# Moving layer 0's projections, and the place of the row maximum in a slot, in a kernel of two cross-attentions

## The chip, the core and the metric

The kernel runs on one core of a Trainium2 chip. The core has five engines, each with an instruction queue of its own that it works off in order: TensorE (PE: matmuls and transposes), VectorE (DVE), ScalarE (ACT), GpSimd (POOL) and SyncE (SP), which here only issues DMAs. They meet through semaphores. The metric is the time of one execution on the device in microseconds (us), the median of several. Three runs of the kernel before gave 1619.97, 1624.86 and 1628.02 us.

## What is computed

Two layers of cross-attention over the same context: 8 batches, 100 queries of width 512, 722 context rows of width 512. Only layer 0 is touched by the change.

```python
# layer 0 (E=512, 16 heads of 32)
qn, kn, vn = layer_norm(query), layer_norm(key), layer_norm(value)      # key = value = context
Q, K, V = (qn @ wq + bq), (kn @ wk + bk), (vn @ wv + bv)                # split into heads
scores = einsum("bqhd,bkhd->bhqk", Q, K) / sqrt(32)
attn = softmax(scores, axis=-1)
out = einsum("bhqk,bkhd->bqhd", attn, V) @ wo + bo
x = query + out
x = x + gelu(layer_norm(x) @ w1 + b1) @ w2 + b2
# layer 1: the same kind of attention with 16 heads of 64, a constant added to the scores,
# then the output projection, the residual and a layer norm
```

## The kernel before

All matmul operands are held as two float16 parts (a high part and what is left), so that a float32 product is three matmuls. The stages follow one another: the queries of layer 0, attention of layer 0, the MLP, the queries of layer 1, attention of layer 1, the output. The change is in the attention of layer 0, function `attention` with `layer == 0`.

A unit of that attention is one batch. The work is a pipeline over steps s = 0 to 9, each of which has, at the same time, the projections of unit s, the scores and softmax of unit s-1, and the last product and the output of unit s-2. A step is cut into 24 slots (`Slots.n`): 4 groups g of 4 heads, with 6 tiles t of context rows each; slot j = 6g + t. The context of unit s+1 is normalised beside it (`ctx_stats`, `ctx_hi`, `ctx_lo`).

What a slot can hold on TensorE:
- `max_scores` (L821), in slots with t < 4: the scores of one head of the NEXT group, 100 queries by 722 keys, two matmuls into the one buffer `p_max`. VectorE reduces them to the row maximum (`take_max`, L1057); the next `max_scores` waits for that reduction (`max_made`). A "row maximum" below is this pair.
- `scores` (L846): four heads of the present group against tile t, into one of two buffers; ScalarE takes the exponential (L954) and casts it to the high part one slot later (L964), GpSimd makes the low part (L649).
- `max_transposes` (L829), at t = 4: turns the four row maxima, which VectorE has split in two parts behind the last reduction (`split_max`, L1064 and L1066), so that VectorE can copy them into the query stack (`place_max`, L1073). The first `scores` of the next group wait for that copy.
- `times_v` (L872, L873), in slots with t from 2 to 5: one head's product of the probabilities of the previous group with V, 12 matmuls.
- `project` (L799 for K, L804 for V): one of 14 projections (a = 0 to 7 for K, 8 to 13 for V), 12 matmuls into one of two buffers `p_proj`. ScalarE evacuates the high part (`evacuate`, L974 or L982), then VectorE the low part (L1081 or L1087); projection a waits until a-2 is evacuated.
- `out_transposes` (L888) in slot 9, for the output of unit s-2; GpSimd makes its low part (L1230) in slot 8.

Nothing is scheduled by a planner: each engine's function `step` writes its queue in this order, slot by slot. The table `at` says in which slot each projection stands, and `Slots.evac` puts its evacuation into the slot behind it on ScalarE and VectorE. SyncE's queue (loads, the stacking of K by DMA in `stack_k`, context transpositions) is written per unit and waits for evacuations by count. Steps 2 to 5 run in a loop of two passes.

Of the kernel before, what the change touches and what calls it, by code (L numbers as in the profile page):

```python
# [28 lines left out]
KT = -(-SK // P)  # L29
# [12 lines left out]
HG = 4  # L42


MAX_T, PV_T = 4, 2
# [433 lines left out]
class Slots:  # L479
# [4 lines left out]
    def __init__(self, layer):  # L484
        self.layer = layer
        self.groups = 4 if layer == 0 else 2
        self.n = KT * self.groups
        self.heads = HG * self.groups

        at = [0, 1, 3, 4, 6, 7, 9, 10, 12, 13, 15, 16, 18, 21] if layer == 0 else [0, 0, 1, 1, 2, 2, 3, 3, 4, 6, 7, 8, 10, 11]  # L490
        self.proj = [[a for a in range(14) if at[a] == j] for j in range(self.n)]

        self.evac = [(self.proj[j - 1][-1:] if j else []) + self.proj[j][:-1] for j in range(self.n)]
        self.evac[-1] = self.evac[-1] + self.proj[-1][-1:]

        self.stat = {t: t for t in range(KT)} if layer == 0 else {}
        self.var_t = KT
        self.ctx = {8: 0, 10: 1, 12: 2, 14: 3, 16: 4, 18: 5} if layer == 0 else {2: 0, 6: 1, 9: 2}
        self.out_t = 9
        self.units = B if layer == 0 else 2 * B  # L500
        self.per = self.units // B
# [29 lines left out]
def attention(nc, layer, ctx_d, q_d, w_k, w_v, kb_col, vb_row, ident, ident16, eps, score_bias, outT,  # L531
# [12 lines left out]
    sl = Slots(layer)  # L544
    NG, NH, U = sl.groups, sl.heads, sl.units
# [11 lines left out]
    with Scope(nc, f"attn{layer}") as sc:  # L557
# [219 lines left out]
        def _(pe):  # L777
# [47 lines left out]
            def max_transposes(s, G1, g):  # L825

                pe.wait_ge(nm_made, G1)
                misc_wait(s, ("max", g), first=(isinstance(s, int) and s == 0))
                pe.transpose(misc16[:, :SQ], nmax_parts[:SQ, :], ident16[:SQ, :SQ]).then_inc(misc_ready, 1)  # L829
# [51 lines left out]
            def out_transposes(s):  # L881

                pe.wait_ge(o_lo_made, s - 1)
                misc_wait(s, ("out", 0))
                for a in range(2):
                    for k in range(ET):
                        o = (a * ET + k) * P
                        last = pe.transpose(misc16[:, o:o + SQ], oparts[:SQ, a, k * P:(k + 1) * P], ident16[:SQ, :SQ])  # L888
                last.then_inc(misc_ready, 1)

            def step(s, par, b, cpar, kind):
                prep, proj, has_scores, outs = kind
                for j in range(sl.n):
                    g, t = divmod(j, KT)
                    if g < NG - 1 and has_scores and t < HG:
                        max_scores(s - 1, 1 - par, g + 1, t)
                    if g == NG - 1 and proj and t < HG:
                        max_scores(s, par, 0, t)
                    if has_scores:
                        scores(s, s - 1, 1 - par, g, t)  # L900
                    if outs and j == sl.out_t:
                        out_transposes(s)
                    if g < NG - 1 and has_scores and t == MAX_T:
                        max_transposes(s, (s - 1) * NG + (g + 2), g)
                    if g == NG - 1 and proj and t == MAX_T:
                        max_transposes(s, s * NG + 1, g)
                    if 0 <= t - PV_T < HG:
                        if g == 0 and outs:
                            times_v(s - 2, par, NG - 1, t - PV_T)
                        if g > 0 and has_scores:  # L910
                            times_v(s - 1, 1 - par, g - 1, t - PV_T)
                    if proj:
                        for a in sl.proj[j]:
                            project(s, par, cpar, a)
# [117 lines left out]
        def _(dve):  # L1032
# [67 lines left out]
            def out_copy(s, par, b):  # L1100
# [3 lines left out]
                out = outT[0 if layer == 0 else par]  # L1104
                dve.tensor_copy(out[:, :, :, bass.ds(b * SQ, SQ)], src).then_inc(misc_freed, 1)

            def step(s, par, b, cpar, kind):
                prep, proj, has_scores, outs = kind
                for j in range(sl.n):
                    g, t = divmod(j, KT)  # L1110
                    if g < NG - 1:
                        nxt = (s - 1, g + 1) if has_scores else None
                    else:
                        nxt = (s, 0) if proj else None
                    if nxt and t < HG:
                        take_max(*nxt, t)
                        if t == HG - 1:
                            if g > 0:
                                prev = sl.misc_count(s, ("max", g - 1)) if has_scores else None
                            else:  # L1120
                                prev = sl.misc_count(s - 1, ("max", NG - 1))
                            split_max(s, *nxt, prev)
                    if layer == 0 and prep:
                        if j in sl.stat:
                            ctx_stats(s + 1, sl.stat[j])
# [22 lines left out]
                    if proj:  # L1148
                        for a in sl.evac[j]:
                            evacuate(s, par, a)  # L1150
                if layer == 1 and has_scores:
                    prob_lo(dve, s - 1, NG - 1, KT - 1)

# [217 lines left out]
```

## Time and profile before

| | before |
|---|---|
| median of three runs | 1624.86 us |
| the profiled execution | 1620.46 us |
| its span, first to last instruction | 1618.7 us |
| mean granted clock of TensorE, share of full | 0.938 |
| TensorE (matmul) busy over the span | 1389.2 us, 86% |
| VectorE busy | 850.4 us, 53% |
| ScalarE busy | 686.2 us, 42% |
| GpSimd busy | 506.6 us, 31% |

Busy time is over the whole program; what holds in one stage is read from the windows and timelines of that stage. The attention of layer 0 takes about 109 to 592 us of the span. In timelines a line gives start, duration, engine, line and operation, and in brackets how long the engine sat idle before it and what ended that. Durations of instructions that follow each other overlap a little, so a sequence is best measured from start to start. A clock of 1.00 is TensorE's full clock (2.4 GHz), 0.50 its lower level (1.2 GHz).

### The profile page before, as it was taken

The numbers are of one execution on the slowest core, as the hardware profiler recorded it, in microseconds if no ns is written. First come the engines' busy times: TensorE is split into PE (matmuls) and PEld (weight loads), VectorE is DVE, ScalarE is ACT, GpSimd is POOL, SyncE is SP. The second block draws the span as 40 slices with busy tenths as digits, with TensorE's granted clock in tenths as the row PEclk, the third lists the DMA queues.
The fourth block names the chain that finished last, engine by engine and source line by source line (L and its number), as shares of the span: only waits on it lengthen the run. The fifth ranks groups of instructions, "written<-read, shape, count | busy, mean of one in ns | idle before, by whom it ended". The sixth has DMA issues, their size and how long they took to land. (4 is left out here: it accounts for less than half of the span.)

```text
span 1618.7 us, 32652 instructions
## 1 busy us (share of the span) xinstructions
PE 1389.2 (86%) x12428; PEld 867.6 (54%) x12428; DVE 850.4 (53%) x1505; ACT 686.2 (42%) x1358; POOL 506.6 (31%) x580
## 2 busy tenths in 40 slices
PE   5467998889899756999938999999999999999968
PEld 3233555556555532544414666666666566666653
DVE  5735677666655637622343455454455455554544
ACT  1323656465555524421222444444444444444441
POOL 3100555455544655020000222222222222221134
PEclk9787999999999767999979999999999999999979
DMA  4275634444432033110286444444454344442221
GB/s 138 56 151 119 132 79 101 105 95 100 103 80 56 28 94 129 53 59 26 87 224 124 99 97 86 101 101 88 81 95 90 77 98 99 103 86 64 56 82 66
DMA packets 217262, 149.97 MB, mean 93 GB/s; under 512 B 148609, under 2 KB 190081, under 8 KB 217105
## 3 DMA queue, kind: packets, MB, share of 16 engines
q1 hardware_dynamic: 217104, 147.81, 39.1%
q8 instruction: 107, 1.75, 0.5%
q14 instruction: 51, 0.41, 0.1%
HBM read 59.29 MB, written 10.65 MB: 43 GB/s over the span
## 5 line engine op out<-in xcount | busy, mean ns | idle before, releaser
L649 POOL TENSOR_TENSOR attn_probs<-attn_p,attn_probs 128x400 f16<-128x400 f32 (+1 forms) x288 | 273.7, 951 | 677.3 <-ACT attn_probs L964 673.2
L1057 DVE TENSOR_REDUCE attn_nmax<-attn_p_max 100x1 f32<-100x722 f32 x256 | 231.7, 905 | 132.8 <-PE attn_p_max L821 130.1
L799 PE MATMUL attn_p_proj<-attn_ctxT,kv_w_k 128*128 128x361 f16 x1536 | 252.4, 319 | 35.0 <-DMA attn_ctxT<-attn_out_o_upper 29.2
L804 PE MATMUL attn_p_proj<-kv_w_v,attn_ctxT 128*128 128x512 f16 (+1 forms) x1152 | 264.3, 379 | 0.0
L954 ACT ACTIVATE attn_p<-attn_p_sc,attn_score_bias 128x400 f32<-128x400 f32 x192 | 113.4, 590 | 288.0 <-PE attn_p_sc L850 287.9
L799 PEld LDWEIGHTS attn_p_proj<-attn_ctxT,kv_w_k 128*128 128x128 f16 x1536 | 144.5, 98 | 122.9 <-DMA attn_ctxT<-attn_out_o_upper 29.6
L964 ACT CAST attn_probs<-attn_p 128x400 f16<-128x400 f32 (+1 forms) x384 | 197.5, 517 | 0.0
L804 PEld LDWEIGHTS attn_p_proj<-kv_w_v,attn_ctxT 128*128 128x128 f16 (+1 forms) x1152 | 110.4, 101 | 111.0
L954 ACT ACTIVATE attn_p<-attn_p_sc 128x400 f32<-128x400 f32 x192 | 95.9, 500 | 171.0 <-PE attn_p_sc L846 168.0
L1087 DVE SCALAR_TENSOR_TENSOR attn_vbuf<-attn_p_proj,attn_vbuf 128x512 f16<-128x512 f32 x144 | 99.4, 690 | 111.8 <-ACT attn_vbuf L982 111.0
L804 PE MATMUL attn_p_proj<-l_w_v,attn_ctxT 128*128 128x512 f16 (+1 forms) x576 | 138.0, 392 | 13.1 <-DVE attn_vbuf L1087 13.1
L799 PE MATMUL attn_p_proj<-attn_ctxT,l_w_k 128*128 128x361 f16 x768 | 134.2, 328 | 9.6 <-DMA attn_ctxT<-attn_cparts 9.4
L1081 DVE SCALAR_TENSOR_TENSOR attn_knat<-attn_p_proj,attn_knat 128x361 f16<-128x361 f32 x128 | 68.3, 534 | 81.9 <-ACT attn_knat L974 81.4
L821 PE MATMUL attn_p_max<-attn_kstack,attn_qstack 96*100 96x361 f16 x256 | 65.9, 340 | 48.9 <-DVE attn_nmax L1057 45.5
L982 ACT ACTIVATE attn_vbuf<-attn_p_proj 128x512 f16<-128x512 f32 x144 | 86.9, 604 | 47.4 <-PE attn_p_proj L804 47.4
L799 PEld LDWEIGHTS attn_p_proj<-attn_ctxT,l_w_k 128*128 128x128 f16 x768 | 73.8, 101 | 50.9 <-issue 13.1
L804 PEld LDWEIGHTS attn_p_proj<-l_w_v,attn_ctxT 128*128 128x128 f16 (+1 forms) x576 | 57.4, 104 | 73.5 <-DVE attn_vbuf L1087 13.6
L849 PE MATMUL attn_p_sc<-attn_qstack_a,attn_kstack_a 128*128 128x100 f16 (+1 forms) x768 | 94.3, 209 | 1.2 <-DVE attn_qstack_b L1073 0.7
L850 PE MATMUL attn_p_sc<-attn_qstack_b,attn_kstack_b 72*128 72x100 f16 (+1 forms) x768 | 94.9, 209 | 0.0
L875 PE MATMUL attn_p_pv<-attn_vbuf,attn_probs 128*128 128x65 f16 (+1 forms) x768 | 86.3, 196 | 2.8 <-DVE attn_probs L649 1.7
L974 ACT ACTIVATE attn_knat<-attn_p_proj 128x361 f16<-128x361 f32 x128 | 60.5, 473 | 64.7 <-PE attn_p_proj L799 64.7
L876 PE MATMUL attn_p_pv<-attn_vbuf,attn_probs 128*128 128x64 f16 (+1 forms) x768 | 86.1, 197 | 0.0
(175 smaller groups left out, 2385.9 us busy)
## 6 DMA issues: line engine op xcount, KB each, us to landing
attn_kstack_a<-attn_knat SPq DMA_DIRECT2D x128, 180.5 KB, 3.7
attn_kstack<-attn_knat SPq DMA_DIRECT2D x192, 90.2 KB, 2.2
attn_kstack_b<-attn_knat SPq DMA_DIRECT2D x64, 180.5 KB, 4.0
attn_c<-in_ctx_dram SPq DMA_DIRECT2D x40, 256.0 KB, 3.6
kernel_w_qo<-in_ctx_dram SPq DMA_DIRECT2D x35, 256.0 KB, 3.2
rows_wo_w<-in_L_xattn_w_dram SPq DMA_DIRECT2D x8, 512.0 KB, 3.8
cols_w_w<-in_L_xattn_w_dram SPq DMA_DIRECT2D x4, 1024.0 KB, 5.6
q_stack<-mlp_hT SPq DMA_DIRECT2D x16, 200.0 KB, 2.8
```

The lines of the kernel that those rows point to most:

```text
L649: eng.tensor_tensor(probs[:r, g % 2, 1, t, :HG * SQ], p32[:r, t % 3, :], probs[:r, g % 2, 0, t, :HG * SQ], ALU.subtract).then_inc(p_lo_mad ...
L799: last = pe.matmul(bank[:, :HALF], w_k[:, wa, k, c0 + m * P:c0 + (m + 1) * P], ctxT[:, cpar, ca, k, n * HALF:(n + 1) * HALF], **flags)
L804: last = pe.matmul(bank[:r, :], ctxT[:, cpar, ca, k, P * t:P * t + r], w_v[:, wa, k, c0:c0 + E], **flags)
L849: pe.matmul(out, kstack[0][:, par, h, P * t:P * t + r], qstack[0][:, par, h, :], start=True, stop=False)
L850: last = pe.matmul(out, kstack[1][:MR + 2 * HG, par, h, P * t:P * t + r], qstack[1][:MR + 2 * HG, par, h, :], start=False, stop=True)
L875: pe.matmul(p_pv[:, o:o + OC], ph, v[:, :OC], start=first, stop=False)
L876: pe.matmul(p_pv[:, o:o + DK], ph, v[:, OC:], start=False, stop=False)
L954: act.activation(p32[:r, t % 3, :], p_sc[:r, t % 2, :HG * SQ], ACT.Exp, bias=bias_col[:r, 0:1] if score_bias else 0.0).then_inc(exp_made, 1)
L964: act.copy(probs[:r, g % 2, 0, t, :HG * SQ], p32[:r, t % 3, :]).then_inc(p_hi_made, 1)
L982: act.activation(vbuf[:r, par, t, :, 0:DK], p_proj[:r, a % 2, :].rearrange("p (h d) -> p h d", d=DK), ACT.Identity, scale=1.0 / WS).then_i ...
L1057: dve.tensor_reduce(nmax[:SQ, hh:hh + 1], p_max[:SQ, :, :HALF], AX.XY, ALU.max, negate=True).then_inc(max_made, 1)
L1087: dve.scalar_tensor_tensor(vbuf[:r, par, t, :, DK + 1:], p_proj[:r, a % 2, :].rearrange("p (h d) -> p h d", d=DK), 1.0 / WS, vbuf[:r, par, ...
```

## The change

Two things change, both for layer 0 only. First, the table `at`: projections stood in slots 0, 1, 3, 4 of a group (the last two in slots 18 and 21), and now stand in slots 0 to 3 of groups 0 and 1 and in slots 0 to 2 of groups 2 and 3. Second, the order inside a slot. On TensorE it was row maximum, scores, transposes, product with V, projection; now it is scores, product with V, transposes, row maximum, projection. On VectorE the reduction of the row maximum stood first in the slot and now stands last, behind the evacuation of a projection. ScalarE and GpSimd keep the order inside a slot; their evacuations move with the table.

```diff
-        at = [0, 1, 3, 4, 6, 7, 9, 10, 12, 13, 15, 16, 18, 21] if layer == 0 else [0, 0, 1, 1, 2, 2, 3, 3, 4, 6, 7, 8, 10, 11]
+        at = [0, 1, 2, 3, 6, 7, 8, 9, 12, 13, 14, 18, 19, 20] if layer == 0 else [0, 0, 1, 1, 2, 2, 3, 3, 4, 6, 7, 8, 10, 11]
...
+            def row_max(s, par, kind, g, t):
+                _prep, proj, has_scores, _outs = kind
+                if g < NG - 1 and has_scores and t < HG:
+                    max_scores(s - 1, 1 - par, g + 1, t)
+                if g == NG - 1 and proj and t < HG:
+                    max_scores(s, par, 0, t)
+
+            def turns(s, kind, j):
+                _prep, proj, has_scores, outs = kind
+                g, t = divmod(j, KT)
+                if outs and j == sl.out_t:
+                    out_transposes(s)
+                if g < NG - 1 and has_scores and t == MAX_T:
+                    max_transposes(s, (s - 1) * NG + (g + 2), g)
+                if g == NG - 1 and proj and t == MAX_T:
+                    max_transposes(s, s * NG + 1, g)
+
             def step(s, par, b, cpar, kind):
                 prep, proj, has_scores, outs = kind
                 for j in range(sl.n):
                     g, t = divmod(j, KT)
-                    if g < NG - 1 and has_scores and t < HG:
-                        max_scores(s - 1, 1 - par, g + 1, t)
-                    if g == NG - 1 and proj and t < HG:
-                        max_scores(s, par, 0, t)
+                    if layer == 1:
+                        row_max(s, par, kind, g, t)
                     if has_scores:
                         scores(s, s - 1, 1 - par, g, t)
-                    if outs and j == sl.out_t:
-                        out_transposes(s)
-                    if g < NG - 1 and has_scores and t == MAX_T:
-                        max_transposes(s, (s - 1) * NG + (g + 2), g)
-                    if g == NG - 1 and proj and t == MAX_T:
-                        max_transposes(s, s * NG + 1, g)
+                    if layer == 1:
+                        turns(s, kind, j)
                     if 0 <= t - PV_T < HG:
                         if g == 0 and outs:
                             times_v(s - 2, par, NG - 1, t - PV_T)
                         if g > 0 and has_scores:
                             times_v(s - 1, 1 - par, g - 1, t - PV_T)
+                    if layer == 0:
+                        turns(s, kind, j)
+                        row_max(s, par, kind, g, t)
                     if proj:
                         for a in sl.proj[j]:
                             project(s, par, cpar, a)
...
+            def maxima(s, kind, g, t):
...
+                if nxt and t < HG:
+                    take_max(*nxt, t)
+                    if t == HG - 1:
...
+                        split_max(s, *nxt, prev)
+
             def step(s, par, b, cpar, kind):
                 prep, proj, has_scores, outs = kind
                 for j in range(sl.n):
                     g, t = divmod(j, KT)
...
+                    if layer == 1:
+                        maxima(s, kind, g, t)
                     if layer == 0 and prep:
                         if j in sl.stat:
                             ctx_stats(s + 1, sl.stat[j])
...
                     if proj:
                         for a in sl.evac[j]:
                             evacuate(s, par, a)
+                    if layer == 0:
+                        maxima(s, kind, g, t)
```

The body of `maxima` is what stood at the head of VectorE's `step`. Line numbers of the changed kernel are higher by 14 to 21 behind the new functions.

TensorE's queue of the kernel before, step 1, from slot 21 (row maximum of t = 3 in group 3) to the transposition of the maxima (L829) in slot 22. L821 is a row maximum, L846 scores, L804 the last V projection; L872 begins one head's product with V, and where rows are left out stand its other eleven matmuls:

```order
L821 MATMUL attn_p_max<-attn_kstack,attn_qstack 100x361 x2
L846 MATMUL attn_p_sc<-attn_qstack,attn_kstack 128x100 x4
L872 MATMUL attn_p_pv<-attn_vbuf,attn_probs 128x65
...
L804 MATMUL attn_p_proj<-l_w_v,attn_ctxT 82x512 x12
L846 MATMUL attn_p_sc<-attn_qstack,attn_kstack 128x100 x4
L829 MATMUL attn_misc<-kernel_ident,attn_nmax_parts 128x100
L872 MATMUL attn_p_pv<-attn_vbuf,attn_probs 128x65
```

The same place in the changed kernel, from slot 20's projection on:

```order
L804 MATMUL attn_p_proj<-l_w_v,attn_ctxT 82x512 x12
L846 MATMUL attn_p_sc<-attn_qstack,attn_kstack 128x100 x4
L872 MATMUL attn_p_pv<-attn_vbuf,attn_probs 128x65
...
L821 MATMUL attn_p_max<-attn_kstack,attn_qstack 100x361 x2
L846 MATMUL attn_p_sc<-attn_qstack,attn_kstack 128x100 x4
L872 MATMUL attn_p_pv<-attn_vbuf,attn_probs 128x65
...
L829 MATMUL attn_misc<-kernel_ident,attn_nmax_parts 128x100
L846 MATMUL attn_p_sc<-attn_qstack,attn_kstack 82x100 x4
```

The V projection that stood between the last row maximum and the transposition now stands in slot 20, ahead of the last row maximum, and slot 22's product has moved ahead of the transposition.

VectorE's queue of the kernel before in step 1, from the evacuation of a V part in slot 13 to that in slot 16 (L1057 reduces a row maximum, L1064 and L1066 split the maxima, L1087 evacuates a V part, L1049 is the context's low part):

```order
L1087 SCALAR_TENSOR_TENSOR attn_vbuf<-attn_p_proj,attn_vbuf 128x16x32
L1057 TENSOR_REDUCE attn_nmax<-attn_p_max 100x1
L1087 SCALAR_TENSOR_TENSOR attn_vbuf<-attn_p_proj,attn_vbuf 128x16x32
L1057 TENSOR_REDUCE attn_nmax<-attn_p_max 100x1
L1064 TENSOR_SCALAR attn_nmax_parts<-attn_nmax 100x4
L1066 SCALAR_TENSOR_TENSOR attn_nmax_parts<-attn_nmax,attn_nmax_parts 100x4
L1049 SCALAR_TENSOR_TENSOR attn_cparts<-attn_c,attn_rstd,attn_cparts 128x512
L1073 COPY attn_qstack<-attn_misc 8x400
L1087 SCALAR_TENSOR_TENSOR attn_vbuf<-attn_p_proj,attn_vbuf 128x16x32
```

And in the changed kernel (L1071, L1078 and L1080, L1101, L1063 and L1087 are the same operations):

```order
L1101 SCALAR_TENSOR_TENSOR attn_vbuf<-attn_p_proj,attn_vbuf 128x16x32
L1071 TENSOR_REDUCE attn_nmax<-attn_p_max 100x1
L1101 SCALAR_TENSOR_TENSOR attn_vbuf<-attn_p_proj,attn_vbuf 128x16x32
L1071 TENSOR_REDUCE attn_nmax<-attn_p_max 100x1
L1063 SCALAR_TENSOR_TENSOR attn_cparts<-attn_c,attn_rstd,attn_cparts 128x512
L1101 SCALAR_TENSOR_TENSOR attn_vbuf<-attn_p_proj,attn_vbuf 128x16x32
L1071 TENSOR_REDUCE attn_nmax<-attn_p_max 100x1
L1078 TENSOR_SCALAR attn_nmax_parts<-attn_nmax 100x4
L1080 SCALAR_TENSOR_TENSOR attn_nmax_parts<-attn_nmax,attn_nmax_parts 100x4
L1087 COPY attn_qstack<-attn_misc 8x400
```

In each slot the reduction has changed places with the evacuation: the last reduction and the splits stand behind the evacuation of slot 14's projection, and behind them there is no evacuation left before the copy.

## Rows read from the trace of the kernel before

**Rows 1.** Windows by step: length, busy us (x instructions) by engine, TensorE's clock, DMA share, GB/s.

```profile
149.00:200.00 51.00, 46.18 (x446) 29.73 (x445) 36.51 (x66) 30.66 (x65) 24.05 (x28) 1.00 0.50 107
200.00:254.20 54.20, 47.97 (x507) 31.64 (x504) 37.45 (x70) 32.05 (x70) 30.09 (x38) 1.00 0.45 107
...
367.20:423.50 56.30, 49.68 (x507) 32.24 (x504) 37.55 (x70) 32.05 (x70) 30.05 (x38) 0.97 0.46 104
...
sum 385.20, PE 340.10 PEld 222.28 DVE 253.73 ACT 219.64 POOL 203.15; mean PE 48.59 PEld 31.75 DVE 36.25 ACT 31.38 POOL 29.02
```

**Rows 2.** What TensorE waited for, 148.9 to 534.2 us: total us, times, longest.

```profile
PE attn_p_max L821 <- DVE attn_nmax L1057: 32.5, 47, 2.1
PE attn_misc L888 <- POOL attn_oparts L1230: 8.1, 6, 1.4
PE attn_p_max L821 <- issue: 3.5, 1, 3.5
```

**Rows 3.** Timeline of TensorE, 370 to 373 us: start, duration, engine, line, operation.

```profile
370.62 2.01 PE L799 MATMUL attn_p_proj<-attn_ctxT,l_w_k 128*128 128x361 f16 x12
372.47 0.48 PE L821 MATMUL attn_p_max<-attn_kstack,attn_qstack 96*100 96x361 f16 x2
```

**Rows 4.** Timeline of TensorE, 408 to 423 us.

```profile
409.89 2.75 PE L804 MATMUL attn_p_proj<-l_w_v,attn_ctxT 128*128 128x512 f16 x12
...
412.48 0.47 PE L821 MATMUL attn_p_max<-attn_kstack,attn_qstack 96*100 96x361 f16 x2
...
417.13 0.51 PE L821 MATMUL attn_p_max<-attn_kstack,attn_qstack 96*100 96x361 f16 x2 [2.11 <-DVE attn_nmax L1057]
...
418.03 4.45 PE L804 MATMUL attn_p_proj<-l_w_v,attn_ctxT 128*82 128x512 f16 x12
422.32 0.34 PE L846 MATMUL attn_p_sc<-attn_qstack,attn_kstack 104*128 104x100 f16 x4
422.50 0.21 PE L829 MATMUL attn_misc<-kernel_ident,attn_nmax_parts 100*128 100x100 f16 x1
```

**Rows 5.** Timeline of VectorE, 408 to 423 us.

```profile
415.57 0.69 DVE L1087 SCALAR_TENSOR_TENSOR attn_vbuf<-attn_p_proj,attn_vbuf 128x512 f16<-128x512 f32 x1 [0.56 <-ACT attn_vbuf L982]
416.18 0.90 DVE L1057 TENSOR_REDUCE attn_nmax<-attn_p_max 100x1 f32<-100x722 f32 x1
417.68 0.91 DVE L1057 TENSOR_REDUCE attn_nmax<-attn_p_max 100x1 f32<-100x722 f32 x1 [0.60 <-PE attn_p_max L821]
...
418.83 0.16 DVE L1066 SCALAR_TENSOR_TENSOR attn_nmax_parts<-attn_nmax,attn_nmax_parts 100x4 f16<-100x4 f32 x1
422.75 0.37 DVE L1073 COPY attn_qstack<-attn_misc 8x400 f16<-8x400 f16 x1 [3.76 <-PE attn_misc L829]
```

**Rows 6.** Timeline of ScalarE, 408 to 423 us.

```profile
414.13 0.48 ACT L954 ACTIVATE attn_p<-attn_p_sc 128x400 f32<-128x400 f32 x1
...
414.93 0.60 ACT L982 ACTIVATE attn_vbuf<-attn_p_proj 128x512 f16<-128x512 f32 x1
...
422.70 0.50 ACT L954 ACTIVATE attn_p<-attn_p_sc 128x400 f32<-128x400 f32 x1 [3.84 <-PE attn_p_sc L846]
```

**Rows 7.** Windows at two falls of TensorE's clock.

```profile
418.60:422.00 3.40, 3.40 (x10) 1.52 (x8) 0.33 (x2) 0.26 (x1) 0.94 (x1) 0.50 0.89 310
445.90:449.30 3.40, 3.40 (x15) 1.78 (x14) 1.26 (x3) 0.00 (x0) 0.00 (x0) 0.50 0.58 117
```

**Rows 8.** Timeline of TensorE, 442 to 476 us.

```profile
444.95 0.53 PE L888 MATMUL attn_misc<-kernel_ident,attn_oparts 100*128 100x100 f16 x8 [1.36 <-POOL attn_oparts L1230]
...
474.78 0.51 PE L821 MATMUL attn_p_max<-attn_kstack,attn_qstack 96*100 96x361 f16 x2 [2.06 <-DVE attn_nmax L1057]
```

**Rows 9.** Timeline of ScalarE in step 0.

```profile
140.19 0.72 ACT L943 ACTIVATE attn_cparts<-attn_c,attn_rstd 82x512 f16<-82x512 f32 x1 [4.23 <-DMA attn_ctxT<-attn_cparts]
```

**Rows 10.** Timeline of TensorE in step 8, which has no projections.

```profile
542.56 0.27 PE L829 MATMUL attn_misc<-kernel_ident,attn_nmax_parts 100*128 100x100 f16 x1
...
544.30 0.78 PE L821 MATMUL attn_p_max<-attn_kstack,attn_qstack 96*100 96x361 f16 x2
```

More of the change, by code:

```diff
@@ L1105, in out_copy @@
                 dve.tensor_copy(out[:, :, :, bass.ds(b * SQ, SQ)], src).then_inc(misc_freed, 1)
+            def maxima(s, kind, g, t):
+                _prep, proj, has_scores, _outs = kind
+                if g < NG - 1:
+                    nxt = (s - 1, g + 1) if has_scores else None
+                else:
+                    nxt = (s, 0) if proj else None
+                if nxt and t < HG:
+                    take_max(*nxt, t)
+                    if t == HG - 1:
+                        if g > 0:
+                            prev = sl.misc_count(s, ("max", g - 1)) if has_scores else None
+                        else:
+                            prev = sl.misc_count(s - 1, ("max", NG - 1))
+                        split_max(s, *nxt, prev)
             def step(s, par, b, cpar, kind):
@@ L1110, in step @@
                     g, t = divmod(j, KT)
[L1111 to L1122, printed above, removed]
+                    if layer == 1:
+                        maxima(s, kind, g, t)
                     if layer == 0 and prep:
```

## The prediction

> **What bounds the kernel now.** I began with the view of spans and clocks (one core, 1618.7 us) and the page's chain of waits, which reaches back over 2% of the span only and says nothing of layer 0. So I cut layer 0 into its steps with the view of windows [rows 1]. Seven steps, from 149.0 to 534.2 us, have both projections and attention; their 385.2 us are what the change can move. The reader should see two things in these rows: TensorE is busy for 340 of the 385 us and no other engine for more than 254, so TensorE bounds the steps; and in the last four of them (one is shown) its granted clock is 0.97, not 1.00. The list of what TensorE waited for [rows 2] says what is left: 32.5 us in 47 waits of a row maximum (L821) for VectorE's reduction of the one before it, 8.1 us in six waits of the output transposes for GpSimd, 3.5 us once at the loop's branch. The timelines of the three engines around 410 to 423 us then show how such a wait comes about [rows 4 to 6].
>
> **Durations, from start to start.** A K projection takes 370.62 to 372.47 = 1.85 us [rows 3], a V projection 409.89 to 412.48 = 2.59, scores 422.32 to 422.50 = 0.18, a row maximum 0.33; a row maximum, scores and the product with V of one head together 417.13 to 418.03 = 0.90, so the product takes 0.37 and scores with product 0.55 [rows 4]. A step's own work on TensorE is 8 x 1.85 + 6 x 2.59 + 24 x 0.18 + 16 x 0.37 + 16 x 0.33 + 0.6 for transposes = 46.5 us. The seven steps, less the branch (3.5) and four falls of the clock at 1.7 us each (below), come to 374.9 us. About 324 is work (the first step lacks four products and the output), so 51 is waiting, 7.3 us per step. That is more than the 41 of the list, since behind each wait some 0.17 us more pass in which the last matmul only drains.
>
> **How a wait arises before.** At 417.13 TensorE had waited 2.11 us: VectorE took a V part at 415.57 and could begin the reduction only at 416.18, and TensorE had 0.55 us of other work between two row maxima [rows 4, 5]. The slots t=2 and t=3 of each group stand so close in each group.
>
> **What the change does.** Three engines get a new order. I walked one full step through it with the durations above, with ScalarE's exponential 0.38 behind the scores' start (422.32 to 422.70), 0.80 for exponential and cast (414.13 to 414.93), 0.64 from the start of its evacuation to VectorE's half (415.57) [rows 4 to 6], VectorE's half 0.61, the reduction 0.91, and 0.40 for the two splits behind it (418.59 to 418.99) [rows 5].
> - Slots with a projection. VectorE now reduces slot j's maximum behind the evacuation of projection j-1, and ScalarE starts that evacuation behind exponential and cast of slot j. From the start of slot j's scores the reduction is done after 0.38 + 0.80 + 0.64 + 0.61 + 0.91 = 3.3 us. A K slot gives TensorE 0.18 + 0.33 + 1.85 + 0.18 = 2.5 us until it wants the next row maximum, with a product 2.9; a V slot 3.3 and more. So K slots still wait, by turns: I get 0.4, 0.6 and 0.7 us in three of the seven, V slots once 0.5.
> - The output transposes now stand behind slot 8's projection. The wait of 1.36 us at 444.95 [rows 8] and its five likes go; the walk counts that.
> - The transposition of the maxima (L829) in slots 16 and 22. Before, a V projection stood behind the row maximum in both slots and ahead of the transposition (418.03 in slot 21 [rows 4]), and VectorE reduced first. Now no projection stands there, and VectorE evacuates slot 14's or 20's before it reduces. From the start of slot 15's scores the split maxima are there after 3.3 + 0.40 + 0.05 = 3.8 us; TensorE has 0.18 + 0.37 + 0.33 + 0.55 = 1.4 us of work. It stands still for **2.4 us, twice in each step**. Queued behind it are scores and products, so ScalarE and GpSimd stand too; nothing is left to cover it. In slots 4 and 10 the projection of slots 3 and 9 covers all but 0.4 and 0.2 us.
> - The first scores of a group wait for the copy of the maxima (0.37 at 422.75, 0.25 behind the transposition's start) against 0.55 of work: 0.2 us with the release, three times a step; at slot 6 0.6, since the statistics of slot 4 stand ahead of the copy.
>
> Per step 2 x 2.4 + (0.4 + 0.6 + 0.7 + 0.5 + 0.4 + 0.2 + 3 x 0.2 + 0.6) = 8.8 us of waiting beside 7.3. The first step has no output, so 44.5 + 8.4 = 52.9; the last has no statistics for the step after, 54.2; five between 55.0 with the work as the walk has it. Together 382.1 beside 374.9: **+7**. Its ends: were VectorE free at the last row maximum, the maxima would be there 1.86 us behind its start (417.13 to 418.99) and TensorE would wait 1.0, not 2.4, which is 14 x 1.4 = 20 less, -13 in all. Were the short waits half as long again (7 x 4.0 / 2 = 14), +21.
>
> **The clock.** In each of the four steps at 0.97 it stands at 0.50, the lower of its two levels (1.2 GHz), once for 3.4 us. It turns the 2.75 us that a V projection is shown with into 4.45 at 418.03, so a fall costs 1.7 us [rows 1, 4, 7]. What TensorE did before the falls: before 418.6 it had waited 2.11 us; before 445.9, 1.36 at the output and a shorter wait ahead of that. But the wait of 2.06 us at 474.78 had no fall behind it [rows 8]. So of two waits over 2 us one was followed by a fall. The change has 14 waits of 2.4 us; at one in two, 7 x 1.7 = 12 us against the three falls of before that do not follow the branch, 5.1. A slowed projection also hides a part of the wait behind it; I take **+5**, with ends -5 (no fall) and +19 (all 14).
> [...]
>
> **The two ends of layer 0.** In step 0 (projections only) ScalarE waits for a context transposition until 140.19 [rows 9] and evacuates the third-last V part behind it; now one projection more and an evacuation stand behind that point ahead of the last reduction: 0 to 2.5 us, I take +1. In step 8 (no projections) a product now runs ahead of the transposition instead of behind it: from 542.56 to the next group's row maximum at 544.30 passed 1.74 us [rows 10], now about 1.4; with an earlier evacuation of the last V part, three groups give -1.5 (0 to -3). SyncE's queue keeps its order: its stacking of K starts up to a slot sooner beside the projections and costs nothing; were that cover gone, the context transposition that ScalarE wants in slot 18 would be late by under 1 us a step, inside the ends above.
>
> Sum: 7 + 5 + 1 - 1.5 = **+11.5 us**. The profiled execution took 1620.46 us (span 1618.7), 4.4 below the median of the runs, 1624.86; on the median this gives **1636 us**.
>
> **Rivals.**
> - Faster, 1607: VectorE is free when the last row maximum of slots 15 and 21 is made, and L829 waits 1.0 us. For it: VectorE is busy for 254 of 385 us only. Against: its order is fixed, and an exponential and a cast stand ahead of what it waits for. 7 - 20 - 5 (no falls) - 0.5 = -18. It decides if L829 waits under 1.3 us. Chance 0.11.
> - Even, 1623: scores that go first let ScalarE run ahead in the other slots, the short waits fall from 4.0 to 2.7 us a step (-9), and the clock falls as often as before (+0): 7 - 9 - 0.5 = about -2. For it: the 2.06 us without a fall. Against: the chain of 3.3 us is longer than a K slot. Chance 0.27.
> - Slower still, 1650: all 14 waits pay 1.7 us, 7 + 19 - 0.5 = +25. For it: a fall in each of the last four steps. Against: none in the first three. Chance 0.12.
> - The forecast with its own range, 1628 to 1645: 0.50.
>
> **How the numbers follow.** Measurements of this kernel tell about 0.5%, 8 us, from no change: faster is below 1617, slower above 1633. The fast rival and a sliver of the even one give faster 0.12; the rest of the even case and the lower edge of the forecast give same 0.30; slower 0.58. The range of 8 in 10 leaves out most of the fast rival and the highest counts of falls: 1614 to 1652.
>
> **What would show it.** Right: 14 waits of L829 of 2.2 to 2.6 us, 30 us and more in the list; the row maxima's 32.5 us down to 15 to 25; the output's 8.1 us gone; more stretches at clock 0.50 in the seven steps, right behind L829. Wrong: waits of about 1 us at L829, a clock of 1.00 in most steps, or seven steps in less than 380 us.

## The result: 1.3% slower, at the waits that were named and with a larger loss to the clock than forecast

The changed kernel takes 1644.2 us (median of 4 runs, 1642.4 to 1646.8) where the kernel before, on the same chip and in the same rounds, takes 1624.0. The ratio is 1.0126, with a 95% interval of 1.0095 to 1.0156: 20 us slower. The forecast was 1636 in a range of 1614 to 1652.

| | before | after |
|---|---|---|
| median | 1623.98 us | 1644.18 us |
| span of the profiled execution | 1618.7 us | 1641.0 us |
| seven steps, from the transposition in slot 22 of step 0 to that of step 7 | 384.3 us | 405.0 us |
| listed waits of TensorE in them, without the loop's branch | 41.5 us | 45.2 us |
| mean granted clock in them | 0.98 | 0.95 |
| busy time of TensorE over the program | 1389.2 us | 1405.9 us |

The seven steps hold 20.7 of the 22.3 us. I cut them at L829 from here on, since that point is in all kernels. They answer to the sum of [rows 1]:

```profile
148.30:553.30 405.00, 355.49 (x3428) 229.88 (x3428) 248.49 (x466) 221.47 (x473) 208.67 (x256) 0.95 0.39 87
```

TensorE's waits in the same stretch answer to [rows 2]:

```profile
PE attn_misc L829 <- DVE attn_nmax_parts L1080: 35.5, 21, 2.4
PE attn_p_max L821 <- DVE attn_nmax L1071: 6.1, 18, 0.7
PE attn_p_sc L846 <- DVE attn_qstack L1087: 3.6, 7, 0.9
PE attn_p_sc L846 <- issue: 3.5, 1, 3.5
```

The 32.5 us at row maxima have become 6.1, the 8.1 us of the output are gone, and 35.5 us stand in 21 waits at L829, which had 0.5 before. The waits changed place, and their sum rose by 3.7 us only.

TensorE's timeline from slot 14's row maximum to slot 18's projection, which answers to [rows 4]:

```profile
418.05 0.49 PE L821 MATMUL attn_p_max<-attn_kstack,attn_qstack 96*100 96x361 f16 x2
418.37 2.75 PE L804 MATMUL attn_p_proj<-l_w_v,attn_ctxT 128*128 128x512 f16 x12
420.96 0.35 PE L846 MATMUL attn_p_sc<-attn_qstack,attn_kstack 104*128 104x100 f16 x4
...
421.51 0.51 PE L821 MATMUL attn_p_max<-attn_kstack,attn_qstack 96*100 96x361 f16 x2
421.86 0.34 PE L846 MATMUL attn_p_sc<-attn_qstack,attn_kstack 104*128 104x100 f16 x4
...
424.95 0.27 PE L829 MATMUL attn_misc<-kernel_ident,attn_nmax_parts 100*128 100x100 f16 x1 [2.38 <-DVE attn_nmax_parts L1080]
...
426.38 0.81 PE L821 MATMUL attn_p_max<-attn_kstack,attn_qstack 96*100 96x361 f16 x2
426.98 3.24 PE L804 MATMUL attn_p_proj<-l_w_v,attn_ctxT 128*128 128x512 f16 x11
```

ScalarE's, answering to [rows 6]:

```profile
421.43 0.50 ACT L968 ACTIVATE attn_p<-attn_p_sc 128x400 f32<-128x400 f32 x1 [1.51 <-PE attn_p_sc L846]
421.83 0.52 ACT L978 CAST attn_probs<-attn_p 128x400 f16<-128x400 f32 x1
422.24 0.62 ACT L996 ACTIVATE attn_vbuf<-attn_p_proj 128x512 f16<-128x512 f32 x1
```

And VectorE's, answering to [rows 5]:

```profile
422.89 0.69 DVE L1101 SCALAR_TENSOR_TENSOR attn_vbuf<-attn_p_proj,attn_vbuf 128x512 f16<-128x512 f32 x1 [0.78 <-ACT attn_vbuf L996]
423.50 0.90 DVE L1071 TENSOR_REDUCE attn_nmax<-attn_p_max 100x1 f32<-100x722 f32 x1
424.43 0.27 DVE L1078 TENSOR_SCALAR attn_nmax_parts<-attn_nmax 100x4 f16<-100x4 f32 x1
424.73 0.16 DVE L1080 SCALAR_TENSOR_TENSOR attn_nmax_parts<-attn_nmax,attn_nmax_parts 100x4 f16<-100x4 f32 x1
425.25 0.37 DVE L1087 COPY attn_qstack<-attn_misc 8x400 f16<-8x400 f16 x1 [0.36 <-PE attn_misc L829]
```

Read across the three: scores at 420.96, exponential 421.43, cast 421.83, ScalarE's half of the evacuation 422.24, VectorE's half 422.89, the reduction 423.50, the two splits, and the transposition at 424.95, 3.99 us behind the scores. The last row maximum had begun at 421.51 and was there 0.51 us later; it lay there for 1.5 us before VectorE came to it. The next row maximum, at 426.38, is followed by a V projection that took 3.24 us for eleven of its matmuls, where twelve had taken 2.75: TensorE's clock had fallen at about 425.0, as the wait ended.

```profile
424.80:428.20 3.40, 3.25 (x26) 2.25 (x27) 2.73 (x6) 1.83 (x4) 1.43 (x3) 0.53 0.73 139
366.80:370.20 3.40, 3.40 (x27) 2.07 (x27) 2.64 (x5) 1.82 (x4) 1.83 (x4) 0.52 0.83 128
245.50:248.90 3.40, 3.40 (x33) 2.07 (x34) 2.95 (x6) 2.45 (x5) 1.76 (x4) 1.00 1.04 130
```

The first two windows begin at the end of a wait of L829 and show TensorE at the lower of its two levels (0.53 and 0.52 as a mean, since the windows' ends are not exactly the stretches'); the third, behind a wait of 2.37 us that ended at 245.42, shows 1.00. The granted clock stands at 0.50 in ten stretches, 44 us in all, where before it was four of 14 us in all. Seven of the ten last 3.4 us; three last 6.8 us, that behind step 0's wait and the two of step 3. One stretch follows step 0's wait at L829, nine follow long waits of steps 2 to 6. Step 7's last wait has one behind it too, which begins step 8. So ten of the 14 long waits have a fall behind them.

### The profile page after: what moved, and what is told of

It is laid out like the page before. It is cut to its first block and busy times, and to the rows that moved or that the text cites. A ratio compares the mean times of both kernels' runs of the same rounds, so it can differ in the third digit from the quotient of the medians.

```text
span 1641.0 us, 32650 instructions
## 1 busy us (share of the span) xinstructions
PE 1405.9 (86%) x12428; PEld 876.8 (53%) x12428; DVE 845.8 (52%) x1505; ACT 688.3 (42%) x1358; POOL 510.9 (31%) x580
## 5 line engine op out<-in xcount | busy, mean ns | idle before, releaser
L1071 DVE TENSOR_REDUCE attn_nmax<-attn_p_max 100x1 f32<-100x722 f32 x256 | 231.6, 905 | 107.1 <-PE attn_p_max L821 104.1
L804 PE MATMUL attn_p_proj<-kv_w_v,attn_ctxT 128*128 128x512 f16 (+1 forms) x1152 | 264.3, 379 | 0.0
L1101 DVE SCALAR_TENSOR_TENSOR attn_vbuf<-attn_p_proj,attn_vbuf 128x512 f16<-128x512 f32 x144 | 99.4, 690 | 149.9 <-ACT attn_vbuf L996 149.7
L804 PEld LDWEIGHTS attn_p_proj<-kv_w_v,attn_ctxT 128*128 128x128 f16 (+1 forms) x1152 | 110.3, 101 | 111.1
L804 PE MATMUL attn_p_proj<-l_w_v,attn_ctxT 128*128 128x512 f16 (+1 forms) x576 | 140.2, 396 | 13.1 <-DVE attn_vbuf L1101 13.1
L799 PE MATMUL attn_p_proj<-attn_ctxT,l_w_k 128*128 128x361 f16 x768 | 139.9, 338 | 9.2 <-DMA attn_ctxT<-attn_cparts 9.1
L799 PEld LDWEIGHTS attn_p_proj<-attn_ctxT,l_w_k 128*128 128x128 f16 x768 | 79.0, 103 | 59.2 <-issue 15.6
L804 PEld LDWEIGHTS attn_p_proj<-l_w_v,attn_ctxT 128*128 128x128 f16 (+1 forms) x576 | 60.8, 106 | 79.4 <-DVE attn_vbuf L1101 13.6
L875 PE MATMUL attn_p_pv<-attn_vbuf,attn_probs 128*128 128x65 f16 (+1 forms) x768 | 86.6, 196 | 3.1 <-DVE attn_probs L649 2.0
L877 PE MATMUL attn_p_pv<-attn_vbuf,attn_probs 128*128 128x65 f16 (+1 forms) x768 | 86.4, 195 | 0.0
```

The source lines that it names most:

```text
L799: last = pe.matmul(bank[:, :HALF], w_k[:, wa, k, c0 + m * P:c0 + (m + 1) * P], ctxT[:, cpar, ca, k, n * HALF:(n + 1) * HALF], **flags)
L804: last = pe.matmul(bank[:r, :], ctxT[:, cpar, ca, k, P * t:P * t + r], w_v[:, wa, k, c0:c0 + E], **flags)
L875: pe.matmul(p_pv[:, o:o + OC], ph, v[:, :OC], start=first, stop=False)
L1071: dve.tensor_reduce(nmax[:SQ, hh:hh + 1], p_max[:SQ, :, :HALF], AX.XY, ALU.max, negate=True).then_inc(max_made, 1)
L1101: dve.scalar_tensor_tensor(vbuf[:r, par, t, :, DK + 1:], p_proj[:r, a % 2, :].rearrange("p (h d) -> p h d", d=DK), 1.0 / WS, vbuf[:r, par, ...
```

## Experiments

Each was run in turn with the kernel before on the same chip. Ratios are to that, with a 95% interval.

| label | ratio | interval | seven steps, us | waits at L821 / L829 / L846 for the copy, us | clock |
|---|---|---|---|---|---|
| the change | 1.0126 | 1.0095 to 1.0156 | 405.0 | 6.1 / 35.5 / 3.6 | 0.95 |
| fill | 1.0026 | 1.0013 to 1.0040 | 392.5 | 9.3 / 10.8 / 3.6 | 0.99 |
| order_only | 1.0240 | 1.0218 to 1.0262 | 426.5 | 49.8 / 0 / 0.6 | 0.94 |
| table_only | 0.9890 | 0.9863 to 0.9916 | 372.9 | 7.8 / 10.8 / 7.8 | 0.99 |
| reduce_first | 0.9976 | 0.9949 to 1.0002 | 385.4 | 1.2 / 16.2 / 17.0 | 0.96 |
| t3_late | 1.0132 | 1.0099 to 1.0165 | 407.1 | 41.8 / 3.1 / 3.6 | 0.96 |
| evac_first | 1.0003 | 0.9987 to 1.0020 | 387.0 | 2.3 / 30.6 / 2.2 | 0.96 |
| t3_reduce_first | 0.9892 | 0.9865 to 0.9920 | 370.3 | 16.5 / 0 / 10.1 | 1.00 |
| t3_old_order | 0.9897 | 0.9871 to 0.9922 | 376.5 | 29.0 / 0 / 2.5 | 0.98 |
| t3_both | 0.9869 | 0.9840 to 0.9899 | 365.3 | 8.2 / 0 / 11.6 | 0.99 |
| table_evac_first | 0.9844 | 0.9815 to 0.9872 | 365.9 | 4.4 / 10.9 / 9.6 | 0.98 |
| t3_old_evac_first | 0.9817 | 0.9791 to 0.9843 | 359.5 | 18.8 / 0 / 2.0 | 1.00 |

### fill: matmuls in the wait, for the clock alone

```diff
+            def fill(u, cpar, a):
+
+                pe.wait_ge(proj_freed, NPROJ * u + (a + 1))
+                for k in range(3 * ET):
+                    pe.matmul(p_proj[:, a % 2, :HALF], w_k[:, 0, k % ET, :P], ctxT[:, cpar, 0, k % ET, :HALF], start=True, stop=True)
...
+                if layer == 0 and proj and t == MAX_T and (g == 3 or g == 2 and has_scores):
+                    fill(s, cpar, 9 if g == 2 else 12)
```

The call stands in `turns`, ahead of `max_transposes`.

> The changed kernel, with 12 further matmuls (128x361, into a projection buffer that is free, result unused) ahead of the transposition of the maxima in slots 16 and 22 of the seven steps. They take 1.85 us of a wait of 2.4 us, so the order and the waits of all other engines stay. Theory A (most of the 20 us is the clock, which falls behind the waits): the falls in the seven steps go, 404.9 us become about 388 and the time about 1627. Theory B (the waits themselves hold TensorE up and the clock is a small part, as the prediction had it with +5): it stays above 1638. Theory C (the filler comes late into the wait and pushes the transposition): over 1650.

1629.85 us, ratio 1.0026: theory A (392.5 and 1630 us, where it said 388 and 1627). The filler (L902) and the transposition behind it:

```profile
412.71 0.35 PE L846 MATMUL attn_p_sc<-attn_qstack,attn_kstack 104*128 104x100 f16 x4
...
414.16 2.00 PE L902 MATMUL attn_p_proj<-attn_ctxT,l_w_k 128*128 128x361 f16 x12
416.70 0.22 PE L829 MATMUL attn_misc<-kernel_ident,attn_nmax_parts 100*128 100x100 f16 x1 [0.53 <-DVE attn_nmax_parts L1088]
```

From slot 15's scores to L829 pass 416.70 - 412.71 = 3.99 us, as in the changed kernel (424.95 - 420.96), and in each of the 14 places the two kernels agree to 0.02 us (3.89 to 3.99 us). So the filler delays nothing and speeds nothing up: the chain through ScalarE and VectorE is as long as before, and what differs is the clock.

```profile
147.90:540.40 392.50, 365.15 (x3597) 237.45 (x3598) 249.79 (x466) 220.85 (x473) 209.12 (x256) 0.99 0.40 90
```

The seven steps are 12.5 us shorter though TensorE is busy 10 us longer, and by the ratios fill is 1.0% (16 us) faster than the change. The time at the lower clock in the seven steps falls by 37 us, from 44 to 7; half of that would be 18.5 us, so about a third of it had been hidden. Some 4 us of that show in the list: without the long ones, the waits are 16 us in fill and were 12 in the change.

The kernel before was not free of the clock either: it spent 14 us at 0.50. The change adds 30 us to that, not 37. At what fill gives back, 12.5 to 16 us for 37, that is an estimate of 10 to 13 of the change's 20 us for the clock, which leaves 7 to 10 for the waits. The list of waits agrees: at full clock the change would have 33 us of long waits and 16 of others, about 49 where before it was 41.5. The 4 us by which fill lies above the kernel before (8 us in the seven steps of the two profiled executions) are less than the waits cost, since fill spends less time at the lower clock than the kernel before.

### table_only and order_only: the two halves of the change

```diff
-        at = [0, 1, 3, 4, 6, 7, 9, 10, 12, 13, 15, 16, 18, 21] if layer == 0 else [0, 0, 1, 1, 2, 2, 3, 3, 4, 6, 7, 8, 10, 11]
+        at = [0, 1, 2, 3, 6, 7, 8, 9, 12, 13, 14, 18, 19, 20] if layer == 0 else [0, 0, 1, 1, 2, 2, 3, 3, 4, 6, 7, 8, 10, 11]
```

table_only is the kernel before with this line; order_only is the changed kernel without it.

> The kernel before with the new table alone; the order inside a slot is the old one on TensorE and VectorE. Theory A (the order on VectorE does the harm, the table helps): a projection now covers each row maximum but the last of groups 2 and 3, the waits at L821 fall from 32.5 to under 10 us, the output's 8.1 us go, L829 waits about 0.8 us in slots 16 and 22; time about 1600. Theory B (three slots without a projection in a row starve TensorE whatever the order): 1635 or more, with waits of 2 us at L829.

> The kernel after with the old table of projections; the order inside a slot is the new one. Theory A: slots t=2 have no projection, and the reduction of t=2 stands behind the evacuation of slot 1's projection; TensorE reaches the row maximum of t=3 1.4 us after the start of slot 2 and the reduction is done after 3.3: 1.9 us of waiting in each of 28 groups, 53 us where 32.5 were, and L829 covered by a projection. Time 1640 to 1655. Theory B (the order alone is harmless and the table does the damage): 1620 or less.

The table alone makes the kernel 1.1% faster (1608.4 us), the order alone makes it 2.4% slower (1665.6 us), more than was expected; both together are 1.3% slower. The signs are those of theory A in both. In the table's kernel:

```profile
PE attn_misc L829 <- DVE attn_nmax_parts L1066: 10.8, 15, 1.4
PE attn_p_max L821 <- DVE attn_nmax L1057: 7.8, 11, 0.8
PE attn_p_sc L846 <- DVE attn_qstack L1073: 7.8, 11, 1.0
```

L829 waits 0.67 us in slots 16 and 22, for the same transposition with the same three slots without a projection. The gain is 18 us, two thirds of the 26 expected. The row maxima (7.8 us) and L829 are as expected; the 7.8 us of the scores for the copy of the maxima were not in the expectation. The order alone shows about the expected 53 us at the row maxima:

```profile
PE attn_p_max L821 <- DVE attn_nmax L1071: 49.8, 41, 2.4
PE attn_misc L888 <- POOL attn_oparts L1251: 9.1, 6, 1.6
```

The longest stand where the slot before has no projection, 2.43 us in slot 15 and 1.68 in slot 3, and in the last group 1.3 and 0.45 us in slots 20 and 21; in slot 9 the output transposes, which stand ahead, wait in their place (L888).

### reduce_first: only VectorE's order undone

```diff
-                    if layer == 1:
-                        maxima(s, kind, g, t)
+                    maxima(s, kind, g, t)
...
-                    if layer == 0:
-                        maxima(s, kind, g, t)
```

> The changed kernel, but VectorE reduces the row maximum first in a slot again, as before the change; the table and TensorE's order are the new ones. Theory A (the 2.4 us at L829 arise because the last reduction stands behind the evacuation of slot 14's and 20's projection): the wait falls to about 1.0 us, the short waits of the row maxima in slots with projections nearly go, the clock falls rarely: 3 to 4 us of waits a step, time about 1595. Theory B (no projection stands ahead of L829, that alone makes the wait): L829 still waits about 2 us and the time stays within 1630 to 1644.

1622.4 us, 0.9976 (not told apart from the kernel before): 22 us better than the change by the medians, so VectorE's order costs about as much as the whole change does. But it is not the expected 1595:

```profile
PE attn_p_sc L846 <- DVE attn_qstack L1087: 17.0, 21, 2.2
PE attn_misc L829 <- DVE attn_nmax_parts L1080: 16.2, 15, 1.4
```

L829 waits 1.0 to 1.1 us in slots 16 and 22, as expected (1.0), but a new 17.0 us stands at the scores that begin a group. Between the splits and the copy of the maxima VectorE now has an evacuation:

```profile
415.36 0.75 DVE L1063 SCALAR_TENSOR_TENSOR attn_cparts<-attn_c,attn_rstd,attn_cparts 128x512 f16<-128x512 f32 x1
416.02 0.68 DVE L1101 SCALAR_TENSOR_TENSOR attn_vbuf<-attn_p_proj,attn_vbuf 128x512 f16<-128x512 f32 x1
416.74 0.37 DVE L1087 COPY attn_qstack<-attn_misc 8x400 f16<-8x400 f16 x1
```

So theory A was right on the cause and wrong on the amount; a wait that is removed at L829 appears in part at the copy, further on in VectorE's queue. Against table_only (1608.4) this kernel has TensorE's new order only, so that order is worth about 14 us to the worse. VectorE's order is the same in both; in TensorE's old order a product stands between L829 and those scores, and they waited 7.8 us instead of 17.0. The clock takes part in it, too: 27 us at 0.50 in the seven steps instead of 10.

### t3_late: the third projection in the slot of the last row maximum

```diff
-        at = [0, 1, 2, 3, 6, 7, 8, 9, 12, 13, 14, 18, 19, 20] if layer == 0 else [0, 0, 1, 1, 2, 2, 3, 3, 4, 6, 7, 8, 10, 11]
+        at = [0, 1, 2, 3, 6, 7, 8, 9, 12, 13, 15, 18, 19, 21] if layer == 0 else [0, 0, 1, 1, 2, 2, 3, 3, 4, 6, 7, 8, 10, 11]
```

> The changed kernel with another table: in groups 2 and 3 the third projection stands in the slot of the last row maximum (15 and 21) and not in slots 14 and 20. The new order inside a slot stays. Theory A (wherever a slot with a row maximum has no projection, the next step of the maxima waits for the 3.3 us chain): L829's waits in slots 16 and 22 go, and the row maxima of slots 15 and 21 wait about 1.9 us each instead; 14 x 0.5 = 7 us better at most, time 1634 to 1642. Theory B (only the place ahead of the transposition matters): the 2.4 us go and nothing comes in their place, time below 1615.

1645.2 us, 1.0132, not told apart from the change. Theory A: 35.5 us at L829 became 3.1, and 6.1 at the row maxima became 41.8. It was expected 2 to 10 us faster and is not. With the reduction behind the evacuation the wait follows the slot that has no projection.

### t3_reduce_first and t3_old_order

> The same table, TensorE's new order, and VectorE reduces first in a slot. Theory A: the row maxima of slots 15 and 21 wait 0.6 us only, L829 is covered, the clock falls rarely; about 1605. Theory B (as with the reduction first and the first table, where the wait went on to the copy of the maxima behind the evacuation, 17.0 us at L846): the copy of the maxima keeps 10 us and more of waits, time about 1615 to 1622.

> The kernel before with the same table and the old order everywhere. With the table of the change and the old order L829 waited 10.8 and L846 for the copy 7.8 us. Theory A: both mostly go, since a projection stands between the last row maximum and the transposition, and the row maxima of slots 15 and 21 wait 0.6 to 1 us (8 to 14 us in all): 1600 to 1608. Theory B (each slot without a projection costs the same wherever it stands): equal to that kernel within its interval, 1608.

1607.6 and 1608.4 us. In the first, the same edit on VectorE as in reduce_first, on top of t3_late, is worth 38 us; waits of 16.5 and 10.1 us remain and the clock is 1.00. In the second, 29.0 us remain at the row maxima, more than the 8 to 14 expected, yet it equals table_only (theory B).

### evac_first: ScalarE evacuates first in a slot

```diff
                     g, t = divmod(j, KT)
+                    if layer == 0 and proj:
+                        for a in sl.evac[j]:
+                            evacuate(s, par, a)
                     if has_scores:
                         exp(s - 1, g, t)
```

> The changed kernel, but ScalarE evacuates a projection first in a slot, ahead of exponential and cast (layer 0 only). Theory A (the 2.4 us at L829 are the chain scores, exponential, cast, evacuation, evacuation, reduction, splits, of which exponential and cast are 1.2): L829 waits about 1.3 us in slots 16 and 22 instead of 2.4, fewer falls of the clock, time about 1622. Theory B (VectorE's own queue makes the wait, ScalarE is early enough): 2.4 us stay and the time stays above 1635. Theory C (exponentials come late and GpSimd's parts with them): new waits of the products for GpSimd.

1626.6 us, 1.0003: near theory A's time, but not by its way, since L829 still waits 2.0 us in each of the 14 places. TensorE's scores of slot 15 and its transposition, and ScalarE's evacuation, in one step:

```profile
412.10 0.35 PE L846 MATMUL attn_p_sc<-attn_qstack,attn_kstack 104*128 104x100 f16 x4
...
415.70 0.22 PE L829 MATMUL attn_misc<-kernel_ident,attn_nmax_parts 100*128 100x100 f16 x1 [2.01 <-DVE attn_nmax_parts L1083]
```

```profile
412.30 0.61 ACT L996 ACTIVATE attn_vbuf<-attn_p_proj 128x512 f16<-128x512 f32 x1 [1.44 <-PE attn_p_proj L804]
```

The evacuation begins 0.20 us behind the scores instead of 1.28 (422.24 - 420.96), but the transposition comes 3.60 us behind them instead of 3.99. The rest went on VectorE, beside GpSimd:

```profile
413.55 0.90 DVE L1074 TENSOR_REDUCE attn_nmax<-attn_p_max 100x1 f32<-100x722 f32 x1
414.48 0.26 DVE L1081 TENSOR_SCALAR attn_nmax_parts<-attn_nmax 100x4 f16<-100x4 f32 x1
414.78 0.86 DVE L1083 SCALAR_TENSOR_TENSOR attn_nmax_parts<-attn_nmax,attn_nmax_parts 100x4 f16<-100x4 f32 x1
```

```profile
413.78 1.84 POOL L649 TENSOR_TENSOR attn_probs<-attn_p,attn_probs 128x400 f16<-128x400 f32 x2 [2.52 <-ACT attn_probs L978]
```

The second split takes 0.86 us and ends at 415.64; GpSimd's two low parts run from 413.78 to 415.62. Over the seven steps its mean is 510 ns, against 163 in the changed kernel:

```profile
L1083 DVE SCALAR_TENSOR_TENSOR attn_nmax_parts<-attn_nmax,attn_nmax_parts 100x4 f16<-100x4 f32 x28 | 14.3, 510 | 1.0
```

```profile
L1080 DVE SCALAR_TENSOR_TENSOR attn_nmax_parts<-attn_nmax,attn_nmax_parts 100x4 f16<-100x4 f32 x28 | 4.6, 163 | 1.0
```

By the Trainium skill, page "SBUF — State Buffer", section "SBUF: two separate sides", a VectorE operation with two SBUF inputs and a GpSimd operation that reads SBUF lock each other out of a shared port pair for a whole instruction. The split reads two tiles in SBUF, and its end at GpSimd's end agrees with that; the reduction, which reads PSUM, kept its 0.90 us in the same stretch. Of the 18 us that the seven steps gain against the change, 6 are in the listed waits (45.2 to 39.3 with the output's) and at most 5 in the clock (44 to 34 us at 0.50); where the other 7 or more lie stays open.

### The faster ones

> Third projection of groups 2 and 3 in slots 15 and 21, VectorE reduces first in a slot, TensorE's new order, and ScalarE evacuates first in a slot. Without the last it took 1607.6 us, with 10.1 us of waits of the scores for the copy of the maxima, which stands on VectorE behind an evacuation. Theory A: an evacuation that is ready 1.1 us sooner lets the copy through, those waits halve and the time falls to 1598 to 1604. Theory B (VectorE's small operations stretch beside GpSimd's when the exponentials move, as with the evacuation first in the changed kernel, where the second split took 510 ns instead of 163): within 3 us of 1607.6.

> The old order inside a slot on TensorE and VectorE, the table of the change, and ScalarE evacuates first in a slot. Without the last it took 1608.4 us, with 10.8 us of waits at L829, 7.8 at L821 and 7.8 for the copy. Theory A: the waits for the copy and at L821 halve, L829 stays (its row maximum is reduced ahead of the evacuation), 1600 to 1605. Theory B: scores wait for exponentials that now come later, no gain, 1608 or more.

> The old order inside a slot on TensorE and VectorE, third projection of groups 2 and 3 in slots 15 and 21, ScalarE evacuates first in a slot. Without the last it took 1608.4 us with 29.0 us of waits at L821, 2.5 for the copy and none at L829. Theory A: the row maxima waited for evacuations that came late from ScalarE; their waits halve and the time falls to 1590 to 1600. Theory B: they wait for the reduction itself (1.48 us from row maximum to row maximum), which stays: 1600 to 1606, no better than the table of the change with the same ScalarE (0.9844).

ScalarE's evacuation first helps the old order: 1601.1 us with the change's table (0.9844), 1598.1 us with the third projection in slots 15 and 21 (0.9817). In the first, the waits at L821 fell from 7.8 to 4.4 us and L829 kept its 10.9, as theory A had it, but those for the copy rose from 7.8 to 9.6. Their intervals overlap, so which of the two is better stays open; both are clear of the kernel before. In the second, which has theory A's time, the row maxima's waits fell from 29.0 to 18.8 us, by a third and not by half:

```profile
PE attn_p_max L821 <- DVE attn_nmax L1060: 18.8, 29, 1.9
...
PE attn_p_sc L846 <- DVE attn_qstack L1076: 2.0, 4, 1.3
```

In t3_both the expected halving of the waits for the copy did not come (10.1 to 11.6 us); those at L821 halved instead (16.5 to 8.2), and the time, 1606.1, is within 3 us of t3_reduce_first (theory B's number, without its cause shown).

## Why the prediction came out as it did

**What bounds.** Right: TensorE's queue bounds the seven steps, and all but 1.6 us of the difference of the two profiled executions arises in them.

**The transposition of the maxima, 2.4 us twice in each step.** Right in place, size and cause. The trace has 2.29 to 2.39 us in the 14 slots; the chain of queues from scores to splits was 3.8 us in the working and 3.99 in the trace. reduce_first shows that VectorE's order makes it: with that order alone undone L829 waits 1.0 to 1.1 us in slots 16 and 22, and in table_only 0.67.

**The short waits, 4.0 us a step.** Too high. 6.1 at L821, 3.6 for the copy and about 2.6 at L829 in slots 4 and 10 make 12 us of listed waits in seven steps, some 18 with the drains, where the working had 28. The row maxima of slots 2, 7, 8 and 13 waited 0.2 to 0.7 us each, as walked, but only two or three of them in a step.

**Waits in sum, +7.** The listed ones rose by 3.7, but slowed work of TensorE hides some of them. With the clock set level the estimate is 7 to 10 us (see fill), so the term was about right. (In the sum five steps stand at 55.0 us where 46.5 + 8.8 is 55.3, 1.5 us in all; the one step of the change between transpositions in slot 16 that had no stretch at 0.50, from 190.37 to 245.42, took 55.05.)

**The clock, +5.** This is the term that was mis-sized. The working took a fall behind one wait in two, from two waits of just over 2 us, and let a part of each be hidden. Ten of 14 had one, three of the ten stretches in the seven steps were twice as long as the 3.4 us it had counted with, and in all 44 us stand against 14: half of the difference is 15 us, and less the third that fill shows to be hidden it is 10, or 13 by the ratios. So the price of a stretch was right, a part was hidden as the working had it, and the number and length of the stretches were too low. The rival that let all 14 fall (+19) was as far off on the other side. The four long waits without a fall, the first three (steps 1 and 2) and one in step 7, are as long as the others (2.29 to 2.37 us); what sets them apart stays open.

**The two ends, -0.5.** In step 0, from the third of the six V projections to the transposition in slot 22 passed 23.0 us instead of 20.8: +2.2, in the bounds of 0 to 2.5. It does not show in the total, as this execution had reached that projection some 3 us earlier. Step 8 was forecast 1.5 us faster; from L829 of step 7 to the next stage passed 54.8 us instead of 54.3. The product ahead of the transposition did help there (from L829 to the next row maximum passed 1.39 us, 562.90 to 564.29, where it was 1.74), but that stretch ran at a mean clock of 0.51 instead of 0.61.

**The rivals.** The fast one asked for L829 under 1.3 us, which the trace denies. The even one had the short waits right (some 2.6 us a step, where it said 2.7) and the clock wrong. The order of the two halves was not in the prediction at all: it weighed the change as one, and did not see that the table alone gains 18 us. The 1644 us lie 8 above the forecast of 1636 and within its range; that is the clock's term for the most part.

## What to carry to other kernels

When two things share a queue, put the one that another engine waits for ahead of the one that waits for another engine itself: here a reduction that TensorE needed stood behind an evacuation that ScalarE had not begun. A wait of TensorE over 2 us costs more than its length when the clock falls behind it, as it did here behind ten of 14. Filler work that fits into the wait shows how much, once the kernel it is compared with has its own time at the lower clock taken into account. Test a table and an order apart; the halves of this change pull in opposite directions.

## What was not expected of the hardware

- Twelve useless matmuls in each long wait (1.85 us of 2.4) took the stretches at the lower clock from 44 us to 7 in the seven steps and the program from 1.0126 to 1.0026 of the time before, with the end of each wait unmoved.
- A 100x4 VectorE operation with both inputs in SBUF took 163 ns on average in one order and 510 ns in another, where it met GpSimd's 128x400 subtraction.
